# The last third of x loaded by SyncE in the loop's beginning instead of by GpSimd at the start, its statistics five slots later

## The chip, the cores and the metric

The kernel runs on one core of one Trainium2 chip. The metric is the device time of one execution in microseconds (us). Five engines work side by side: TensorE (PE; its weight loads are PEld), VectorE (DVE), ScalarE (ACT), GpSimd (POOL) and SyncE (SP), which here only issues DMAs. Each engine has its own program and waits for the others through semaphores. DMAs issued by SP travel in queue q1, those of ACT in q10, those of GpSimd in q0; all are carried by the core's 16 DMA engines.

## The reference, cut to what matters

x has 32 batches of 100 query rows of 256 values, the context 32 batches of 361 rows of 256.

```python
x = x + LN(z + LN0(x)) * gamma + beta      # z: 16-head cross attention of LN0(x) on ctx
x = x + FFN(LN0(x))                        # a second LN, top-2 of 8 experts (256-512-256, gelu), FFN adds its own input
LN0(x) = (x - mean(x)) / sqrt(var(x) + 1e-5)
```

What the change touches is the first LN0: every batch's rows of x must be in SBUF, and their mean and variance over 256 values computed, before the batch's queries are projected and, again, before its residual is added.

## The kernel before

Attention runs batch by batch as one software pipeline. A turn `i` has twelve slots `s` (`NG`), and in every slot each engine issues its share of up to five batches at once: batch i+3 is projected (keys L835, normalised rows L1099 and their transpose L845, queries L853), batch i+1 gets its value projection (L866), its score rows (L880) and their maxima (VectorE, L1344), batch i its transposed scores (L899), exponentials (L1163), a guard on VectorE (L1349) and the product with the values (L911); i-1 and i-2 get the end of attention and its layer norm. `pipeline()` runs i from -3; tables such as `DVE_PLACE` say in which slot a step stands. After the 32 batches, routing and the expert tiles follow (from about 560 us on).

Scores are computed in bfloat16 from a sum of products of parts. For each batch the queries and the keys are split into three parts (high on ACT, rest on GpSimd, middle on ACT, low on GpSimd: L748 to L771), and six DMAs each copy the parts into stacks of 96 rows: `q_stack<-q_part` (L624, for batch 0 L1238 on ACT) and `stack_x<-k_part` (L630). The stacks' last rows hold the row maxima, also in three parts; SyncE copies them there (L614) before the transposed scores (L899) of that batch. That copy is issued once per batch, from `m_part`, which ACT fills from a TensorE transpose (L890) of the parts `m_rows`.

x_all, behind the key stacks in the tensor `stack_x`, holds all of x. Four loads fill it (`X_LOADS`): batches 0 to 3 by ACT at the very start, 4 to 11 by SyncE behind the first weights and contexts (L589), 12 to 21 and 22 to 31 by GpSimd (L670), one behind the other, after the inverse deviations of batches 0 to 3. VectorE takes statistics (`x_sums`, one bn_stats a batch, L1280) and eight small steps turn them into a variance (`x_variance_step`, L1290 to L1304); GpSimd raises it to the power of -0.5 (`inverse_deviation_x`, L666), VectorE makes the offset (`x_offset`, L1313). This is done in three parts (`X_PARTS`): batches 0 to 3 before turn -3, 4 to 21 at the end of turn -2, and 22 to 31 in turns 0 to 2: the ten statistics stand one each in slots 0 to 9 of turn 0, the eight small steps in slots 1 to 8 of turn 1, the power at the end of GpSimd's turn 1, the offset at the end of turn 2. ACT waits for that offset before turn 4.

SyncE's program in its order: the first weights and contexts, L589, then for turn -3 batch 0's key stack copies, for turn -2 batch 1's query copies. At the start of turn -1 stands `later_loads()`: gamma and beta (L594, wanted by GpSimd in turn 2) and b1 (L595). The places of SyncE's table put batch 1's key copies (`k`, place 11) into turn -2 and so ahead of `later_loads()`. Behind it, in turn -1, stands the context of batch 3 (L607, wanted by the key projection in slot 5 of turn 0), in turn 0 the copy of batch 0's maxima (L614), and then batch 2's query and key copies.

Of the kernel before, what the change touches and what calls it, by code (L numbers as in the profile page):

```python
# [12 lines left out]
B, Q, D = 32, 100, 256  # L13
# [12 lines left out]
NG = G * KT  # L26
TINY = 1e-30
FIRST = 4
X_LOADS = [slice(0, FIRST), slice(FIRST, 12), slice(12, 22), slice(22, B)]
X_LATE = 22  # L30
TAIL_FROM = B - 2
X_PARTS = [slice(0, FIRST), slice(FIRST, X_LATE), slice(X_LATE, B)]
SCORES_LAG, GUARD_LAG, VALUES_LAG = 3, 6, 9
# [44 lines left out]
def after(eng, sem, value):  # L78

    if isinstance(value, int) and value <= 0:  # L80
        return
    eng.wait_ge(sem, value)


def lagging(turn, i, s, lag):

    return Batch(turn, i + (s - lag) // NG), (s - lag) % NG
# [13 lines left out]
def span_of(n, offset):  # L101

    if n.known and offset < 0 and n.index >= TAIL_FROM:
        return "tail"
# [24 lines left out]
def occupant_before(users, name, n):  # L129

    def at(user, index):
        offset, place = users[user]
        if n.known and offset < 0 and index >= TAIL_FROM:
            place = TAIL["PE"].get(user, place)
# [22 lines left out]
def build(nc, x, ctx_t, wq_t, bq, wk_t, bk, wv_t, bv, gamma, beta, ln_g, ln_b, rw, rb, w1, b1, w2, b2,  # L157
          ident_d, route_c, zscr, zf_d, odd_d, out):
    es = ExitStack()
    with es:  # L160
        def sem(name):
            return es.enter_context(nc.semaphore(name))
# [11 lines left out]
        x_all = stack_x[0:Q, stack_words:].rearrange("q (b d) -> q b d", b=B)  # L174
# [16 lines left out]
        x_loaded = [sem(f"x_loaded{k}") for k in range(4)]  # L191
# [272 lines left out]
        with att:  # L464
# [111 lines left out]
            def _(sp):  # L576
# [13 lines left out]
                sp.wait_ge(pad_written, 3)  # L590

                def later_loads():
                    for dst, src in zip(row_c, (gamma, beta)):
                        sp.dma_start(dst[:], src.unsqueeze(0).broadcast_to([Q, D])).then_inc(tail_const, 16)  # L594
                    sp.dma_start(b1_s[:], b1).then_inc(b1_loaded, 16)  # L595

                def iteration(turn, i):
                    if isinstance(turn, int) and i == -1:
                        later_loads()
# [52 lines left out]
            def _(pool):  # L652
# [10 lines left out]
                def inverse_deviation_x(k):  # L663

                    pool.wait_ge(ln0_step, 8 * (k + 1))
                    g.tensor_tensor(rstd0[:, X_PARTS[k]], ln0[0][:, X_PARTS[k]], half[:, 0:1].broadcast_to([Q, X_PARTS[k].stop - X_PARTS[k].start]), ALU.pow).then_inc(rstd0_ready, 1)  # L666

                inverse_deviation_x(0)
                for k in (2, 3):
                    pool.dma_start(x_all[:, X_LOADS[k], :], x.rearrange("b q d -> q b d")[:, X_LOADS[k], :]).then_inc(x_loaded[k], 16)  # L670

                gathers = [pool.alloc_register(f"gathers{k}") for k in range(2)]
                scatters = [pool.alloc_register(f"scatters{k}") for k in range(2)]
# [588 lines left out]
            def _(dve):  # L1262
# [15 lines left out]
                def x_sums(batches):  # L1278
                    for b in batches:
                        v.bn_stats(stats0[:, b, :], x_all[:, b, :]).then_inc(stats0_done, 1)  # L1280

                def x_variance_step(k, n):
                    part = X_PARTS[k]
                    me, mo = stats0[:, part, 1], stats0[:, part, 4]
                    l0, l1, l2 = (t[:, part] for t in ln0[0:3])
                    if n == 0:
                        dve.wait_ge(stats0_done, part.stop)
                    after(dve, ln0_step, 8 * k + n)
                    if n == 0:
                        v.tensor_tensor(l0, me, mo, ALU.add).then_inc(ln0_step, 1)  # L1290
                    elif n == 1:
                        v.tensor_scalar(mean0[:, part], l0, 0.5, None, ALU.mult).then_inc(ln0_step, 1)
                    elif n == 2:
                        v.tensor_tensor(l0, me, mo, ALU.subtract).then_inc(ln0_step, 1)
                    elif n == 3:
                        v.tensor_tensor(l1, l0, l0, ALU.mult).then_inc(ln0_step, 1)
                    elif n == 4:
                        v.tensor_tensor(l2, stats0[:, part, 2], stats0[:, part, 5], ALU.add).then_inc(ln0_step, 1)
                    elif n == 5:
                        v.tensor_scalar(l1, l1, 0.25, EPS, ALU.mult, ALU.add).then_inc(ln0_step, 1)  # L1300
                    elif n == 6:
                        v.tensor_scalar(l2, l2, 1.0 / D, None, ALU.mult).then_inc(ln0_step, 1)
                    else:
                        v.tensor_tensor(l0, l2, l1, ALU.add).then_inc(ln0_step, 1)  # L1304
# [168 lines left out]
                def iteration(turn, i):  # L1473
                    for s in range(NG):
# [6 lines left out]
                        n, g = lagging(turn, i, s, GUARD_LAG)  # L1481
# [4 lines left out]
                        if isinstance(turn, int) and i == -3 and s == 0:  # L1486
# [2 lines left out]
                            pad_stack(q_stack[ROWS:128].rearrange("r s h k -> r (s h k)"))  # L1489
                            for k in (1, 2):  # L1490
                                pad_stack(k_stack[ROWS:128, k].rearrange("r h k -> r (h k)"))
                        if isinstance(turn, int) and i == 0 and s < B - X_LATE:
                            if s == 0:
                                dve.wait_ge(x_loaded[3], 16)
                            x_sums(range(X_LATE + s, X_LATE + s + 1))
                        if isinstance(turn, int) and i == 1 and 1 <= s < 9:
                            x_variance_step(2, s - 1)
                        if isinstance(turn, int) and (i, s) == (-1, 0):
                            dve.wait_ge(route_const, 64)
                            for c in range(2):  # L1500
# [58 lines left out]
                        b = Batch(turn, i + 1)  # L1559
# [102 lines left out]
```

## Time and profile before

| | us |
|---|---|
| median of 3 runs | 878.26 (876.82 to 878.76) |
| the profiled execution | 875.23 |
| its span | 873.4 |
| TensorE busy | 751.5 (86%) |
| VectorE busy | 671.9 (77%) |
| GpSimd busy | 560.0 (64%) |
| ScalarE busy | 534.7 (61%) |

The span is the time between the first and the last instruction of the profiled execution; 1.8 us of its own time lie around it. Busy shares are means over the whole span. The page also cuts the span into 40 slices of 21.8 us and gives, for each, the busy tenths of every engine, TensorE's granted clock in tenths (PEclk, 9 being nearly full) and the DMA engines' share. A wait is charged to what ended it.

### The profile page before, as it was taken

Reading aid. Unit: us, or ns where it says so; the run is one execution under the profiler, and the core shown is the slowest. Engines: PE = TensorE matmul, PEld = TensorE weight load, DVE = VectorE, ACT = ScalarE, POOL = GpSimd, SP = SyncE. Lnnn points to the kernel's source line nnn. Section 1 sums busy time; section 2 is a strip of 40 time slices with the busy share of each in tenths; the row PEclk is TensorE's granted clock in tenths of the full one; section 3 lists DMA queues with packets and bytes.
Section 4 is the critical chain, followed back from the end, with each engine's and each line's share of the span. In section 5 each row is a group of like instructions: output and inputs, shape, how many; then the busy total and the mean of one; then the engine's idle time right before and its main releaser. Section 6 shows DMA issues by size and latency. Waiting matters only on the chain.

```text
span 873.4 us, 26128 instructions
## 1 busy us (share of the span) xinstructions
PE 751.5 (86%) x8056; PEld 584.9 (67%) x8057; DVE 671.9 (77%) x1855; ACT 534.7 (61%) x1412; POOL 560.0 (64%) x611
## 2 busy tenths in 40 slices
PE   3389999999999999999999988538786889999970
PEld 1256677777777777777777655427676779998960
DVE  7389999999999999999999977883468755555630
ACT  3246787888878888888887864425444345554520
POOL 6323877777777787777778754343755567777840
PEclk9699999999999999999999988757999999999995
DMA  8755576676776767758677687512342244443327
GB/s 198 141 131 121 129 166 151 161 172 149 175 163 148 180 152 165 173 139 188 138 176 164 154 247 204 142 34 43 60 60 43 45 67 68 67 61 57 64 36 150
DMA packets 154502, 110.95 MB, mean 127 GB/s; under 512 B 68688, under 2 KB 147884, under 8 KB 153920
## 3 DMA queue, kind: packets, MB, share of 16 engines
q1 hardware_dynamic: 132598, 77.01, 38.9%
q0 software_dynamic: 12192, 19.43, 13.5%
q10 hardware_dynamic: 9658, 13.85, 5.1%
q8 instruction: 28, 0.46, 0.2%
q14 instruction: 26, 0.21, 0.1%
HBM read 39.90 MB, written 23.88 MB: 73 GB/s over the span
## 4 chain that ended last, share of the span: by engine, by line
PE 62%; DVE 14%; issue 7%; DMA 5%; DVEq 4%; POOL 4%; ACT 1%; ACTq 1%; POOLq 0%; SPq 0%
PE pj L866 9%; PE pj L835 9%; PE s_row L880 9%; PE zt L911 8%; PE s_t L899 8%; PE s_row L970 5%; DVE negmax L1344 3%; PE pj L853 3%; PE zt L981 2%; PE pj L981 2%; DMA q_stack<-q_part 2%; DVE v_neg L1446 1%; DVEq L1441 1%; DVEq L1433 1%; PE tr L935 1%
## 5 line engine op out<-in xcount | busy, mean ns | idle before, releaser
L1344 DVE TENSOR_REDUCE negmax<-s_row 100x1 f32<-100x361 f32 x512 | 251.5, 524 | 25.9 <-PE s_row L880 18.9
L1163 ACT ACTIVATE p_t<-s_t 128x400 f32<-128x400 f32 x384 | 188.7, 501 | 61.7 <-PE s_t L899 55.4
L880 PE MATMUL s_row<-stack_x,q_stack 125*128 125x361 bf16 x512 | 133.2, 323 | 14.5 <-DMA q_stack<-q_part 7.9
L899 PE MATMUL s_t<-q_stack,stack_x 128*128 128x100 bf16 x1536 | 129.6, 212 | 14.7 <-ACT p_t L1163 10.5
L899 PEld LDWEIGHTS s_t<-q_stack,stack_x 128*128 128x128 bf16 x1536 | 93.6, 100 | 61.8 <-issue 27.0
L970 PE MATMUL s_row<-w_qkv,v_aug 128*128 128x128 f32 x912 | 115.6, 281 | 15.4 <-DVE v_aug L1435 15.4
L970 PEld LDWEIGHTS s_row<-w_qkv,v_aug 128*128 128x128 f32 x912 | 109.5, 197 | 18.4 <-DVE v_aug L1435 16.5
L866 PE MATMUL pj<-w_qkv,ct 128*128 128x256 f32 x384 | 107.4, 403 | 0.0
L835 PE MATMUL pj<-ct,w_qkv 128*128 128x361 f32 x256 | 94.9, 494 | 10.3 <-DMA bk_s<-in_bk 9.2
L1149 ACT ACTIVATE w_qkv<-s_row,b_k 128x128 f32<-128x128 f32 x228 | 64.9, 368 | 62.5 <-PE s_row L970 62.5
L1349 DVE TENSOR_SCALAR p_t<-p_t 128x1200 f32<-128x1200 f32 x128 | 100.9, 789 | 0.3 <-ACT p_t L1163 0.2
L911 PE MATMUL zt<-p_t,v_aug 128*32 128x100 f32 (+1 forms) x3072 | 97.4, 260 | 1.7 <-DVE p_t L1349 1.0
L911 PEld LDWEIGHTS zt<-p_t,v_aug 128*32 128x32 f32 (+1 forms) x3072 | 67.7, 112 | 28.8 <-issue 24.9
L688 POOL DMA_INDIRECT q_part<-zf_d,idx_g x57 | 64.4, 1130 | 22.8 <-issue 15.0
L880 PEld LDWEIGHTS s_row<-stack_x,q_stack 125*128 125x128 bf16 x512 | 48.1, 102 | 45.8 <-DVE negmax L1344 25.4
L698 POOL DMA_INDIRECT out_x<-v_neg,idx_s x29 | 49.9, 1719 | 35.4 <-DVE v_neg L1448 25.7
L866 PEld LDWEIGHTS pj<-w_qkv,ct 128*128 128x128 f32 x384 | 67.4, 195 | 6.2
L698 POOL DMA_INDIRECT odd_d<-v_neg,idx_s x28 | 48.2, 1723 | 29.8 <-DVE v_neg L1448 22.8
L776 POOL TENSOR_TENSOR u<-z_in,td 100x256 f32<-100x256 f32 x32 | 45.9, 1433 | 31.0 <-DMA z_in<-zscr 21.2
L835 PEld LDWEIGHTS pj<-ct,w_qkv 128*128 128x128 f32 x256 | 45.5, 196 | 27.2 <-issue 10.4
L1435 DVE TENSOR_SCALAR v_aug<-w_s 128x1024 f32 x57 | 40.4, 708 | 27.2 <-issue 24.9
L779 POOL TENSOR_TENSOR rstd<-var,half 100x1 f32<-100x1 f32 x32 | 33.1, 1035 | 43.8 <-DVE var L1384 43.8
(234 smaller groups left out, 1482.1 us busy)
## 6 DMA issues: line engine op xcount, KB each, us to landing
stack_x<-k_part SPq DMA_DIRECT2D x192, 192.0 KB, 3.8
q_stack<-q_part SPq DMA_DIRECT2D x186, 64.0 KB, 2.0
ct<-in_ctx_t SPq DMA_DIRECT2D x32, 361.0 KB, 5.0
stack_x<-in_w ACTq DMA_DIRECT2D x8, 512.0 KB, 6.4
w_s<-in_w ACTq DMA_DIRECT2D x14, 256.0 KB, 3.1
zscr<-zn SPq DMA_DIRECT2D x32, 100.0 KB
z_in<-zscr SPq DMA_DIRECT2D x32, 100.0 KB
zf_d<-zf_s SPq DMA_DIRECT2D x32, 100.0 KB
```

The lines of the kernel that those rows point to most:

```text
L688: pool.indirect_dma_start(zg[:, k.ring, :], None, zf_rows[0:n], bass.IndirectOffsetOnAxis(idx_g[:, k.ring:k.ring + 1], 0), bounds_check=n ...
L698: pool.indirect_dma_start((out_rows, odd_rows)[k.slot][0:n], bass.IndirectOffsetOnAxis(idx_s[:, k.slot:k.slot + 1], 0), ys[:, k.slot, :], ...
L835: last = nc.tensor.matmul(pj[1][:, 0:KEYS], wk_s[:, c, t * 128:t * 128 + 128], ct[:, a.slot, c, 0:KEYS], start=(c == 0), stop=(c == 1))
L866: last = nc.tensor.matmul(bank[:, kt % 2 * D:kt % 2 * D + D], ct[:, b.slot, c, kt * 128:kt * 128 + 128], wv_s[:, c, :], start=(c == 0), st ...
L880: nc.tensor.matmul(s_row[h % 2][:, 0:KEYS], q_stack[0:MROW, b.slot, h, :], k_stack[0:MROW, b.slot, h, 0:KEYS], start=True, stop=True).then ...
L899: last = nc.tensor.matmul(s_t[g % 2][:, j * Q:j * Q + Q], k_stack[:, b.slot, h, kt * 128:kt * 128 + 128], q_stack[:, b.slot, h, 0:Q], star ...
L911: last = nc.tensor.matmul(zt[32 * j:32 * j + 32, quad * Q:quad * Q + Q], v_aug[0:n, b.slot, kt * H + 4 * quad + j, :], p_t[0:n, quad % 2, ...
L970: last = nc.tensor.matmul(p_h[k.slot][:, j * 128:j * 128 + 128], w1_k[k.slot][:, c * HF + j * 128:c * HF + j * 128 + 128], zgt[:, k.slot, ...
L1149: nc.scalar.activation(hidt[:, k.slot, j * 128:j * 128 + 128], p_h[k.slot][:, j * 128:j * 128 + 128], ACT.Gelu, bias=b1_k[:, k.slot, j:j + ...
L1163: nc.scalar.activation(p_t[:, quad % 2, kt, :], s_t[g % 2][:, 0:4 * Q], ACT.Exp).then_inc(exp_done, 1)
L1344: v.tensor_reduce(negmax[:, b.slot, h:h + 1], s_row[h % 2][0:Q, 0:KEYS], AXIS.X, ALU.max, negate=True).then_inc(max_done, 1)
L1349: v.tensor_scalar(p_t[:, quad % 2], p_t[:, quad % 2], 0.0, None, ALU.max).then_inc(p_ready, 1)
```

## The change

Load 3 (x of batches 22 to 31, 1000 KB) is issued by SyncE as the first thing of `later_loads()`, no longer by GpSimd. Its ten statistics and the wait for the load move from slots 0 to 9 of turn 0 to slots 5 to 11 of turn 0 and 0 to 2 of turn 1. The eight small steps move from slots 1 to 8 to slots 4 to 11 of turn 1. GpSimd's power and the offset stay at the ends of turns 1 and 2.

```diff
+X_SLOT = 5
...
                 def later_loads():
+                    sp.dma_start(x_all[:, X_LOADS[3], :], x.rearrange("b q d -> q b d")[:, X_LOADS[3], :]).then_inc(x_loaded[3], 16)
                     for dst, src in zip(row_c, (gamma, beta)):
...
                 inverse_deviation_x(0)
-                for k in (2, 3):
-                    pool.dma_start(x_all[:, X_LOADS[k], :], x.rearrange("b q d -> q b d")[:, X_LOADS[k], :]).then_inc(x_loaded[k], 16)
+                pool.dma_start(x_all[:, X_LOADS[2], :], x.rearrange("b q d -> q b d")[:, X_LOADS[2], :]).then_inc(x_loaded[2], 16)
...
-                        if isinstance(turn, int) and i == 0 and s < B - X_LATE:
-                            if s == 0:
+                        if isinstance(turn, int) and 0 <= i * NG + s - X_SLOT < B - X_LATE:
+                            n = X_LATE + i * NG + s - X_SLOT
+                            if n == X_LATE:
                                 dve.wait_ge(x_loaded[3], 16)
-                            x_sums(range(X_LATE + s, X_LATE + s + 1))
-                        if isinstance(turn, int) and i == 1 and 1 <= s < 9:
-                            x_variance_step(2, s - 1)
+                            x_sums(range(n, n + 1))
+                        if isinstance(turn, int) and i == 1 and 4 <= s < 12:
+                            x_variance_step(2, s - 4)
```

## Rows read from the trace of the kernel before

**Rows 1.** The page: span, busy times, TensorE's granted clock in 40 slices.
```profile
span 873.4 us, 26128 instructions
PE 751.5 (86%) x8056; PEld 584.9 (67%) x8057; DVE 671.9 (77%) x1855; ACT 534.7 (61%) x1412; POOL 560.0 (64%) x611
```

**Rows 2.** Timeline, 29 to 60 us: start, duration, engine, line, operation [idle before <-releaser].
```profile
29.24 3.37 DVE L1280 BATCH_NORM_STATS2 stats<-stack_x 100x6 f32<-100x256 f32 x10 [7.98 <-DMA stack_x<-in_x]
...
34.87 3.30 POOL L666 TENSOR_TENSOR rstd<-ln,half 100x18 f32<-100x18 f32 x1 [0.97 <-DVE ln L1304]
...
41.51 0.78 PE L880 MATMUL s_row<-stack_x,q_stack 125*128 125x361 bf16 x2 [7.93 <-DMA q_stack<-q_part]
...
42.21 3.81 SPq L630 DMA_DIRECT2D stack_x<-k_part  x6
...
47.49 0.60 SPq L607 DMA_DIRECT2D ct<-in_ctx_t  x1
...
55.47 0.47 PE L880 MATMUL s_row<-stack_x,q_stack 125*128 125x361 bf16 x2
...
56.80 0.85 SPq L614 DMA_DIRECT2D q_stack<-m_part  x1
...
59.11 0.53 PE L899 MATMUL s_t<-q_stack,stack_x 128*128 128x100 bf16 x8
```

**Rows 3.** ACT's six query stack copies of batch 0 (L1238), issue to landing.
```profile
DMA to landing us min/median/max: 8.2/11.3/15.7
```

**Rows 4.** DMA queues, 14 to 18, 18 to 22, 22 to 26 us: packets, MB, share.
```profile
q0 software_dynamic: 233, 0.32, 46.0%
...
q0 software_dynamic: 165, 0.68, 101.5%
...
q0 software_dynamic: 205, 0.55, 103.3%
q1 hardware_dynamic: 6, 0.01, 3.8%
```

**Rows 5.** GpSimd's two loads of x (L670), from their issue at 10.8 and 13.5 us.
```profile
DMA to landing us min/median/max: 18.4/21.8/25.2
```

**Rows 6.** DMA queues, 38 to 41.5 us.
```profile
DMA packets 542, 0.36 MB, mean 103 GB/s; under 512 B 65, under 2 KB 541, under 8 KB 541
```

**Rows 7.** Busy us by stretch: PE, PEld, DVE, ACT, POOL, granted clock, DMA share, GB/s.
```profile
41.50:47.30 5.80, 5.74 (x16) 3.74 (x16) 3.23 (x7) 0.34 (x1) 0.68 (x1) 0.51 0.71 165
...
59.10:68.00 8.90, 7.11 (x76) 4.55 (x75) 8.79 (x22) 4.87 (x13) 1.66 (x2) 1.00 0.79 182
68.00:75.00 7.00, 7.00 (x72) 5.02 (x69) 5.95 (x12) 5.37 (x14) 3.95 (x5) 1.00 0.18 48
```

**Rows 8.** The context load of batch 3 (L607), issue to landing.
```profile
DMA to landing us min/median/max: 4.5/4.5/4.5
```

**Rows 9.** DMA traffic, 12.5 to 15 (batches 4 to 11 of x), 43 to 52, 50 to 51.5 us.
```profile
DMA packets 475, 0.38 MB, mean 153 GB/s; under 512 B 104, under 2 KB 475, under 8 KB 475
...
q1 hardware_dynamic: 371, 0.38, 69.6%
...
DMA packets 1500, 1.77 MB, mean 197 GB/s; under 512 B 276, under 2 KB 1500, under 8 KB 1500
...
DMA packets 333, 0.35 MB, mean 235 GB/s; under 512 B 92, under 2 KB 333, under 8 KB 333
```

**Rows 10.** TensorE's timeline: a value projection at the low and the high clock.
```profile
42.09 1.91 PE L866 MATMUL pj<-w_qkv,ct 128*128 128x256 f32 x4
...
54.60 1.03 PE L866 MATMUL pj<-w_qkv,ct 128*128 128x256 f32 x4
```

**Rows 11.** Timeline, 83 to 88 us, VectorE and GpSimd.
```profile
83.32 0.39 DVE L1304 TENSOR_TENSOR ln<-ln 100x10 f32<-100x10 f32 x1
...
87.21 2.49 POOL L666 TENSOR_TENSOR rstd<-ln,half 100x10 f32<-100x10 f32 x1
```

## The prediction

> **What bounds the kernel now.** I read the page first: TensorE is busy 86% of a span of 873.4 us, and its 40 slices are full but for the first ones [rows 1]. A batch in the steady part is out of reach of a load that runs once, so only the start can change. I then read the timeline of the first 100 us, the landings and the DMA queues in short windows.
>
> TensorE's score rows of batch 0 start at 41.51 us, after 7.93 us of waiting for the copies of q_part into q_stack [rows 2]. ACT's six copies take 8.2 to 15.7 us to land [rows 3]. The cause stands in the queues: from 18 to 26 us the engines carry GpSimd's queue at 101.5 and 103.3%, SyncE's at 3.8% in the second half, where its stack copies are issued [rows 4]. Of GpSimd's two loads of 1000 KB one lands after 18.4 us (the ten statistics at 29.24 show it) and the other after 25.2 us, near 38.7 [rows 2, 5]. The second is the load that the change moves. From 38 to 41.5 us only 103 GB/s flow [rows 6]: the few engines that still shared their time with that load work off their copies.
>
> The next thing is which wait ends last *after* 41.5 us. Batch 1's score rows begin at 55.47, and the first transposed scores of batch 0 at 59.11; SyncE issues the small copy of the maxima that these wait for at 56.80 [rows 2]. VectorE is busy 8.79 of 8.9 us from 59.1 on and sets the pace there; then TensorE does, 7.00 of 7 us [rows 7].
>
> **The change part by part.** The sum is against the profiled execution, 875.23 us; the median of the three runs is 878.26, 3.0 higher, and I carry the difference over to it.
>
> *Load 3 leaves the beginning.* Both loads together are 2.05 MB; GpSimd's queue moved 0.32 MB from 14 to 18 us and 0.68 in the next 4 [rows 4]. Alone, load 2 has 0.7 MB left at 18 us: 4 to 8 us, so it lands at 22 to 26, not 29.2. The last of batch 0's twelve stack copies was issued 15.7 us before 41.4, at 25.7. They then have the engines to themselves and land near 34 to 35 (bounds 33 and 38): the first score row starts 6 to 7 us earlier. GpSimd's issue of 2.2 us goes too, on an engine that then idles.
>
> *What of that reaches batch 1.* Its key copies are issued at 42.21, behind the chain: ten statistics, eight small steps, GpSimd's power of 18 columns (34.87, 3.30 us), k_rest, k_mid, k_low [rows 2]. GpSimd had waited 0.97 us for the steps. With load 2 early the power starts at 33.9, 1.0 us earlier, and no more, since what GpSimd does ahead of it hangs on ACT, which issues copies until 26.4. So batch 1's key copies go out at 41.2.
>
> *Load 3 in SyncE's queue.* It is 1.02 MB ahead of gamma, beta, b1, batch 3's context and, as it turns out, the copy of batch 0's maxima. SyncE's own issue grows by about 0.5 us, hidden, since the queue behind is backlogged. The context load goes out at 47.49 and lands 4.5 us later, at 52.0 [rows 2, 8]; the queue is empty until 56.80. The trace doesn't show this load in this place, so I bound it: at the 235 GB/s of the end of that backlog 4.4 us; at the 153 GB/s of the load of batches 4 to 11, same form and queue, 6.7 us [rows 9]. The whole backlog ran at 197, which gives 5.2. I take 6.0, nearer to the load of the same form. Then the context lands at 52.0 - 1.0 + 6.0 = 57.0 and the small copy, issued near 50 now, right behind it, about 57.4. The key copies of batch 1, ahead of load 3, land by about 49 (the context behind them in before landed at 52.0), and the slots from batch 1's first score row to those scores took 3.6 us (55.5 to 59.1), so TensorE would be ready at 52 to 53. So the start's 6 to 7 us shrink to 59.1 - 57.4 = 1.7 us.
>
> Against the change speaks that the load of batches 4 to 11 held the engines at 69.6% only, the work of 11 of 16 [rows 9]: SyncE's load doesn't use them all, so the full-width rates may not hold for it.
>
> The Trainium skill (DMA: Bandwidth & Descriptors, "Why a DMA increments its semaphore by 16 and not by 1") says that a load issued from SyncE runs on the largest number of engines up to 16 that divides its slowest dimension, so ten for 100 partitions, and those the lowest. The trace agrees within one engine. By the rule with the backlog's rate, ten sixteenths of 197 GB/s, the load would take 8.3 us and the sum below would be +1.4 us.
>
> *The new idle time of TensorE.* It waits some 5 us before 57.4. After 7.9 us without a matmul the granted clock was at its low level of 1.2 GHz (0.51), for 5.8 us of work, and 1.00 from 59.1 on [rows 2, 7]. At the low level two value projections (x4) took 1.91 us, at the high one 1.03 [rows 10]; score rows suffer less, so I take 1.7 times. In 3 to 5.8 us of low clock that adds 1.3 to 2.4 us to the 7.11 us of TensorE work of that stretch: 8.4 to 9.5 against 8.9 [rows 7].
>
> *The statistics.* Ten take 3.37 us, 0.34 each [rows 2]. Five leave slots 0 to 4 of batch 0's turn; five go to slots 10, 11 and the first three of the next turn. In the stretch from 59.1 VectorE loses two of them, 0.7 us, and what it still owed at 59.11, an estimated 1.2 us (two row maxima and a bias add): 6.9 of its 8.79 are left [rows 7], so TensorE sets that stretch. I take +0.2 us for it, with the clock. From 68 to 75 us VectorE idles 1.05 us and gets up to 1.7 us of statistics, less the first small steps, which move on: I take 0.3 us for what finds no gap there.
>
> *The small steps, three slots later.* The last one ran at 83.32, and GpSimd's power of ten columns started at 87.21, held by nothing but its order [rows 11]. Now the last step stands in slot 11, three slots on, about 87.5 at some 1.4 us a slot, so the power starts about 0.3 us later, with k_rest behind it: +0.3.
>
> Sum: -1.7 + 0.2 + 0.3 + 0.3 = -0.9 us: 874.3 for the profiled execution, 877.4 for the median. A difference under 0.2% (1.75 us) is what a measurement of this kernel can't tell from none.
>
> **The rivals.**
>
> *The start's gain survives (faster).* If the maxima's copy isn't held behind load 3, the scores start near 53 and 6 us are kept, less 0.6 for the rest: 872.9. If it is held but load 3 takes only 4.4 us, the head gains 3.3, the idle time is shorter, and about 2.5 us are kept: 875.8. For it speaks the full rate after the backlog; against the first form, that every copy of SyncE before 52.0 landed in the order of issue.
>
> *The wait moves and brings the low clock (slower).* Its place is TensorE's wait for the maxima's copy. At 69.6% of the backlog's 197 GB/s load 3 takes 7.5 us and the head gains only 0.2; TensorE then idles over 6 us and has the low clock for 6 us of work or more, which costs 2 us in place of 0.2: 878.3 - 0.2 + 2.0 + 0.6, about 880.7. It decides from 7 us of load 3 on, or from a low clock longer than 6 us.
> The Trainium skill's rule on the number of engines (DMA: Bandwidth & Descriptors, the section named above) speaks for this rival.
>
> *Nothing to gain, since the engines carry the same bytes.* The stack copies run on the same engines, so taking 1.02 MB from one place and putting it in another gives back later what it gives now: 878.3. From the rows it needs a first score row still near 38 and a context load later by all of 6 us.
> The Trainium skill has it as a rule (DMA: Bandwidth & Descriptors, "Issuing engines are not separate DMA queues"): queues of several engines interleave on the same 16, and another issuer saves its issue time alone. From 22 to 26 us the trace doesn't agree: SyncE's queue has copies to carry and gets 3.8%.
>
> **How the numbers follow.** My forecast and the third rival both end within 0.2%: 0.42. The first rival: 0.38, most of it in its second form and in shifts of a microsecond that fall on that side. The second: 0.20. The range takes the bounds: 4.4 us for load 3 with little clock loss gives 874; a bit of the surviving start takes it to 873.5; 7.5 us and the long low clock end at 880.6.
>
> **What would show it.** Right: the first score row near 34 to 35; batch 1's key copies issued near 41; load 3 issued behind them; the maxima's copy issued near 50 but landing near 57; TensorE idle from 52 on, waiting for that copy; a second stretch of low granted clock after it; batch 4's k_rest 0.3 us late behind the power. Wrong: a first score row still at 38 or later; scores of batch 0 starting within 2 us of the issue of the maxima's copy; a granted clock of 1.00 through 50 to 70 us, which with a short load 3 would make it clearly faster; statistics that wait for load 3.

## The result, and the profile after

The change made the kernel slower, by a little. The median is 878.15 us over 22 runs (875.89 to 879.82), that of the kernel before, run beside it, 876.16 (869.13 to 878.76): a ratio of 1.0032, 95% interval [1.0018, 1.0046]. A second set gave 1.0056 [1.0035, 1.0078]. The forecast was 0.1% faster (877.4). The profiled execution took 879.75 us.

The page after: span and busy times; only the span moved [rows 1].
```profile
span 877.9 us, 26128 instructions
...
PE 754.9 (86%) x8056; PEld 587.6 (67%) x8057; DVE 670.7 (76%) x1855; ACT 534.8 (61%) x1412; POOL 558.3 (64%) x610
```

The timeline after, 25 to 65 us, with the columns of [rows 2]:
```profile
26.03 3.37 DVE L1281 BATCH_NORM_STATS2 stats<-stack_x 100x6 f32<-100x256 f32 x10 [4.82 <-DMA stack_x<-in_x]
...
34.98 0.47 PE L881 MATMUL s_row<-stack_x,q_stack 125*128 125x361 bf16 x2
...
42.76 1.22 SPq L632 DMA_DIRECT2D stack_x<-k_part  x2
...
46.61 0.54 SPq L594 DMA_DIRECT2D stack_x<-in_x  x1
...
49.63 0.60 SPq L609 DMA_DIRECT2D ct<-in_ctx_t  x1
...
51.15 0.85 SPq L616 DMA_DIRECT2D q_stack<-m_part  x1
...
53.09 0.47 PE L881 MATMUL s_row<-stack_x,q_stack 125*128 125x361 bf16 x2
...
59.71 0.85 PE L900 MATMUL s_t<-q_stack,stack_x 128*128 128x100 bf16 x8 [6.15 <-DMA q_stack<-m_part]
...
61.82 2.77 PE L836 MATMUL pj<-ct,w_qkv 128*128 128x361 f32 x4 [0.66 <-DMA ct<-in_ctx_t]
```
Read it from the top. Load 2 is in 3.2 us earlier (26.03 for 29.24), the first score row starts 6.5 us earlier. Then load 3 goes out at 46.61, the context of batch 3 and the copy of the maxima behind it, and TensorE stands from 53.6 to 59.7, waiting for that 9.4 KB copy. Before, it had those scores at 59.11. A gain of 6.5 us has become a loss of 0.6.

The landing of the contexts loaded in the loop (L609) after: the longest is batch 3's, 12.1 us where it took 4.5 [rows 8].
```profile
DMA to landing us min/median/max: 4.0/4.9/12.1
```

Busy times by stretch after, columns of [rows 7] (the granted clock is the third from the end):
```profile
54.00:58.00 4.00, 0.00 (x0) 0.00 (x0) 0.76 (x2) 0.00 (x0) 0.00 (x0) 0.73 0.81 210
58.00:62.00 4.00, 1.63 (x11) 0.98 (x12) 1.10 (x3) 1.14 (x3) 0.00 (x0) 0.50 1.12 230
62.00:66.00 4.00, 4.00 (x15) 2.19 (x15) 0.94 (x3) 0.60 (x2) 0.00 (x0) 0.50 0.98 204
66.00:70.00 4.00, 3.42 (x38) 2.16 (x41) 4.00 (x10) 3.15 (x9) 0.57 (x1) 0.99 0.11 30
```
The clock's low level falls on the first work after the wait. GpSimd's timeline after, 87 to 92 us, where [rows 11] had the power at 87.21:
```profile
88.57 1.01 POOL L740 TENSOR_TENSOR m_rows<-m_rest,m_rows 100x16 bf16<-100x16 f32 x1
89.88 2.42 POOL L668 TENSOR_TENSOR rstd<-ln,half 100x10 f32<-100x10 f32 x1 [0.31 <-DVE ln L1305]
```

The power now waits 0.31 us for the last small step, as expected; of its 2.7 us of delay 2.2 are the delay of the whole pipeline (batch 2's maxima are transposed at 89.99 for 87.75).

The ledger. These starts, in us, are read from TensorE's timelines of the profiled executions; "in the gap" is the kernel *gap_late* of the experiments.

| start of | before | change | in the gap |
|---|---|---|---|
| first score row | 41.5 | 35.0 | 34.7 |
| batch 0's transposed scores | 59.1 | 59.7 | 53.0 |
| transpose of batch 1's maxima | 71.9 | 74.4 | 65.4 |
| of batch 3's maxima | 104.4 | 107.6 | 98.6 |
| of batch 31's maxima | 549.8 | 552.1 | 544.0 |
| end of the span | 873.4 | 877.9 | 868.1 |

Change against before: +0.6 at the scores, +2.0 up to batch 1's maxima, +0.7 over the next two batches, -0.9 over the other 28. That last figure is spread between traces: the second traces of both kernels have 445.1 us there. The expert part has +2.2 us, and that too is not the change's: it comes in two lengths, about 324 and 326 us from batch 31's maxima to the end. The change had 325.8 in one trace and 324.2 in another, the kernel before 323.6 and 325.9.

### The profile page after: what moved, and what is told of

The parts are those of the page before. It is cut to its first block, busy times and chain, and to the rows that moved or that the text cites. A ratio compares the mean times of both kernels' runs of the same rounds, so it can differ in the third digit from the quotient of the medians.

```text
span 877.9 us, 26128 instructions
## 1 busy us (share of the span) xinstructions
PE 754.9 (86%) x8056; PEld 587.6 (67%) x8057; DVE 670.7 (76%) x1855; ACT 534.8 (61%) x1412; POOL 558.3 (64%) x610
## 4 chain that ended last, share of the span: by engine, by line
PE 62%; DVE 13%; issue 7%; DMA 6%; POOL 4%; DVEq 4%; ACT 2%; SPq 1%; ACTq 1%; POOLq 0%
PE pj L836 9%; PE pj L867 9%; PE s_row L881 8%; PE zt L912 8%; PE s_t L900 8%; PE s_row L971 6%; PE pj L854 3%; PE pj L982 3%; DVE negmax L1345 2%; PE zt L982 2%; DMA q_stack<-m_part 1%; DVE v_neg L1447 1%; DMA ct<-in_ctx_t 1%; DVEq L1434 1%; DVEq L1442 1%
## 5 line engine op out<-in xcount | busy, mean ns | idle before, releaser
L1164 ACT ACTIVATE p_t<-s_t 128x400 f32<-128x400 f32 x384 | 188.5, 501 | 68.4 <-PE s_t L900 62.5
L971 PE MATMUL s_row<-w_qkv,v_aug 128*128 128x128 f32 x912 | 118.0, 285 | 13.7 <-DVE v_aug L1436 13.7
L971 PEld LDWEIGHTS s_row<-w_qkv,v_aug 128*128 128x128 f32 x912 | 111.7, 200 | 16.7 <-DVE v_aug L1436 14.9
L836 PE MATMUL pj<-ct,w_qkv 128*128 128x361 f32 x256 | 96.3, 500 | 10.9 <-DMA bk_s<-in_bk 9.1
L867 PE MATMUL pj<-w_qkv,ct 128*128 128x256 f32 x384 | 104.8, 395 | 0.5 <-ACT k_rest L1087 0.5
L777 POOL TENSOR_TENSOR u<-z_in,td 100x256 f32<-100x256 f32 x32 | 48.1, 1504 | 30.5 <-DMA z_in<-zscr 21.3
L836 PEld LDWEIGHTS pj<-ct,w_qkv 128*128 128x128 f32 x256 | 46.0, 198 | 28.8 <-issue 10.9
L765 POOL TENSOR_TENSOR k_rest<-k_rest,k_part 128x722 f32<-128x722 f32 x32 | 51.7, 1614 | 16.0 <-ACT k_rest L1087 16.0
```

The costliest lines, as they stand in the source:

```text
L836: last = nc.tensor.matmul(pj[1][:, 0:KEYS], wk_s[:, c, t * 128:t * 128 + 128], ct[:, a.slot, c, 0:KEYS], start=(c == 0), stop=(c == 1))
L867: last = nc.tensor.matmul(bank[:, kt % 2 * D:kt % 2 * D + D], ct[:, b.slot, c, kt * 128:kt * 128 + 128], wv_s[:, c, :], start=(c == 0), st ...
L971: last = nc.tensor.matmul(p_h[k.slot][:, j * 128:j * 128 + 128], w1_k[k.slot][:, c * HF + j * 128:c * HF + j * 128 + 128], zgt[:, k.slot, ...
L1164: nc.scalar.activation(p_t[:, quad % 2, kt, :], s_t[g % 2][:, 0:4 * Q], ACT.Exp).then_inc(exp_done, 1)
```

## The experiments

Theory A: the start's gain is real, and load 3 gives it back, since its packets hold the engines that the maxima's copy and batch 3's context need next; the loss beyond zero comes from those two waits and the low clock behind them. Rivals: the order of SyncE's queue alone; the late statistics and the late power; the clock. In the first expectations theory A goes by the name of bytes theory, and the order of SyncE's queue by that of ring theory. In the cuts of the edits "..." stands for lines left out; wherever load 3 gets a new line, its line in `later_loads()` goes. All ratios are to the kernel before, run on the same chip, with 95% intervals.

### The change a second time


> The changed kernel itself, on the chip of the next three. Ring theory (load 3 stands ahead of batch 3's context and of batch 0's maxima copy in SyncE's queue): as in the first profile, transposed scores of batch 0 near 59.7 us though their copy is issued near 51, a low granted clock from 56 to 66 us, and 1.002 to 1.005 of the kernel before. Statistics theory (the later statistics cost the time): the same ratio. Bytes theory (the 16 engines carry the same bytes, wherever they are issued): the same ratio.

878.59 us, 1.0056 [1.0035, 1.0078]. Transposed scores of batch 0 at 60.8, the transpose of batch 1's maxima at 74.8, of batch 3's at 108.0: the pattern repeats. Its first score row stands at 37.7, not 35.0; what made that is told in the last section.

### Statistics alone
Both loads back on GpSimd, everything else as changed:
```diff
-                    sp.dma_start(x_all[:, X_LOADS[3], :], ...)
...
-                pool.dma_start(x_all[:, X_LOADS[2], :], ...)
+                for k in (2, 3):
+                    pool.dma_start(x_all[:, X_LOADS[k], :], ...)
```


> The kernel before with the change's statistics and small steps in their later slots alone; both loads stay with GpSimd. In the change and in three other kernels with late small steps, batch 3's maxima are transposed 17.5 to 17.6 us after batch 2's, where the kernel before has 16.6. If the later small steps delay GpSimd's power and key rest of batch 4 (statistics theory, as one part), the same interval shows 17.6 here, with the head as before (first transposed scores at 59), and the ratio is 1.001. If the interval came from the shifted loads, it stays at 16.6 and the ratio is 0.999 to 1.000.

874.43 us, 0.9999 [0.9977, 1.0022]. The late statistics and steps cost nothing that shows in the time. Batch 0's scores to batch 3's maxima take 45.0 us here (55.88 to 100.86) and 45.2 in both traces of the kernel before. The loss is load 3's.

### Load 3 behind the maxima's copy
```diff
+                        if isinstance(turn, int) and (i, s) == (-1, 7):
+                            sp.dma_start(x_all[:, X_LOADS[3], :], ...)
...
-X_SLOT = 5
+X_SLOT = 8
...
```
The small steps start two slots later, two at a time at first.

> Load 3 still issued by SyncE, but behind batch 3's context and batch 0's maxima copy; statistics from slot 8 of turn 0. Ring theory: the context lands near 52, the maxima copy within 3 us of its issue at 51, transposed scores of batch 0 near 53 to 54, no low clock after 50 us, and 5 to 6 us less than the kernel before: ratio 0.993 to 0.995. Bytes theory: load 3 then delays batch 2's stack copies or something else by as much, so the ratio stays at 1.000 or above. Statistics theory: they are later still, so 1.003 or more.

875.81 us, 1.0031 [1.0005, 1.0057]. TensorE's timeline, 52 to 70 us:
```profile
52.97 0.53 PE L901 MATMUL s_t<-q_stack,stack_x 128*128 128x100 bf16 x8
...
64.04 0.35 PE L901 MATMUL s_t<-q_stack,stack_x 128*128 128x100 bf16 x4 [1.46 <-ACT p_t L1165]
...
69.11 0.76 PE L882 MATMUL s_row<-stack_x,q_stack 125*128 125x361 bf16 x2 [2.85 <-issue]
```
The copy lands at 53.0, 2.3 us after its issue, and the scores start 6.7 us sooner than in the change. But load 3, now in flight from 52 to 62, holds batch 2's stack copies: the last of its key copies lands at 69.0, where TensorE's next score row starts (the trace calls that wait "issue"). The wait has moved one batch on.

### Load 3 from ACT's queue
```diff
+                        if isinstance(turn, int) and (i, s) == (-1, 9):
+                            act.dma_start(x_all[:, X_LOADS[3], :], ...)
...
```


> Load 3 issued by ACT in slot 9 of turn -1 (near 45 us), in a queue of its own, with SyncE's queue as in the kernel before. Ring theory: it shares the engines packet by packet and holds nobody up for its whole length: batch 3's context lands by 54 to 55, the maxima copy within 3 us of its issue, scores of batch 0 at 53 to 55, ratio 0.993 to 0.997. Bytes theory: same bytes at the same time as in the change, so the copy waits as long and the ratio is 1.003. Statistics theory: 1.003.

878.03 us, 1.0052 [1.0030, 1.0075]. SyncE's queue holds no load 3, yet TensorE waits longer than in the change. Its timeline, and the DMA queues from 50 to 60 us:
```profile
62.21 0.85 PE L899 MATMUL s_t<-q_stack,stack_x 128*128 128x100 bf16 x8 [8.76 <-DMA q_stack<-m_part]
```
```profile
q1 hardware_dynamic: 1250, 0.97, 44.0%
q10 hardware_dynamic: 961, 0.98, 39.5%
```
The two queues share the engines, and both are slower for it: load 3's thousand packets, issued at 47.7, were in flight for 11.2 us (51.0 to 62.2), and batch 3's context took 12.2 us to land.

### The maxima's copy from ACT's queue
```diff
...
+                            if b.known and b.index == 0:
+                                act.wait_ge(m_copied, 1)
+                                act.dma_start(q_stack[MROW:MROW + 3, 0, :, 0:Q], m_part[:]).then_inc(m_stacked[0], 16)
```


> The change, with the small copy of batch 0's maxima issued by ACT (which has just written m_part) instead of by SyncE; load 3 stays where the change has it. Theory A (load 3's thousand packets of 1 KB keep the ten lowest engines busy whatever queue the copy travels in, as the load in ACT's queue suggested): the copy still lands near 58 to 62, TensorE's wait of 6 us stays, batch 1's maxima at 73.5 to 75, ratio 1.002 to 1.006. Theory B (the copy is held by the order of SyncE's queue): it lands near 54, the transposed scores start near 54 to 55, batch 3's context, still behind the load, then ends a wait near 60, ratio 0.998 to 1.002.

879.10 us, 1.0042 [1.0022, 1.0061]. The timeline, 50 to 61 us:
```profile
50.31 0.85 ACTq L1221 DMA_DIRECT2D q_stack<-m_part  x1
...
60.49 0.85 PE L902 MATMUL s_t<-q_stack,stack_x 128*128 128x100 bf16 x8 [7.78 <-DMA q_stack<-m_part]
```
A copy of 9.4 KB, alone in its queue, takes 10 us. (SyncE, which no longer waits for the maxima, issues batch 2's query copies from 49.46 instead of 52.05, so a little more competes with it than in the change.) With the run before, the order of SyncE's queue falls as the cause: what counts is what the engines already hold, whichever queue it came from. Here the Trainium skill's rule (DMA: Bandwidth & Descriptors, "Issuing engines are not separate DMA queues") agrees with the traces: another issuer brings no other carrier.

### Load 3 as 96 and 4 partitions
```diff
+                    for rows in (slice(0, 96), slice(96, Q)):
+                        sp.dma_start(x_all[rows, X_LOADS[3], :], ...)
...
```


> The change with load 3 as two DMAs of SyncE, of 96 and 4 partitions. If the load's 8 us are those of ten engines carrying 100 packets each (partitions 100), the first part spreads over 16 and takes about 5 us: the maxima copy lands 2 to 3 us earlier (56.5 to 57.5), and the ratio falls by 0.002 to 0.004, to about 1.000. If the memory side sets the 145 GB/s of the load, its length stays at 8 us and the ratio at 1.003.

876.61 us, 1.0037 [1.0018, 1.0056]; batch 1's maxima are transposed at 73.1, 1.7 us before the change run beside it. The trace's semaphore events tell how many engines carried a load. Uncut, load 3 leaves ten landings in the first trace of the change, from 56.2 to 58.1 us; the piece of 96 partitions leaves sixteen, from 54.3 to 55.0. The uncut load shows in the context behind it too: six of its sixteen landings come at 53.5 to 53.8, the other ten from 58.3 on. So load 3 sits on ten engines. Spreading it makes it about 2 us shorter (its last four partitions land at 56.4) but puts it in front of everything on all sixteen: the maxima's copy still landed at 59.4, for 59.7 and 60.7 in the two traces of the change. Against the change run beside it 1.3 of the 1.7 us are that wait (59.45 for 60.76) and 0.4 the stretch behind it, where the context came at 60.0, not 62.5. The two traces of the change differ by as much from each other, and the ratios overlap, so no gain of the cut is shown.

### Matmuls in place of the wait
```diff
...
+                        for _ in range(FILL):
+                            nc.tensor.matmul(s_t[1][:, 0:KEYS], q_stack[0:ROWS, 0, 0, :], k_stack[0:ROWS, 0, 0, 0:KEYS], start=True, stop=True)
```


> The change with 32 extra matmuls on TensorE (into a bank that the next scores overwrite) while it waits for batch 0's maxima copy. Clock theory: the granted clock stays at 1.00 from 50 to 70 us, transposed scores start near 59.7 as in the change, but batch 1's maxima are transposed 1.5 to 2 us earlier than in it (near 73) and the ratio falls by 0.002 against the change. If the wait alone costs the time, batch 1's maxima stay near 74.7 and the ratio stays at 1.003 to 1.005.

1.0034 [1.0015, 1.0053], and it told nothing: TensorE still waited 1.43 and 1.28 us, and the clock fell all the same, from 62 to 69 us. Mended, with 36 before the scores and 14 before batch 3's key projection:

> The change, with 36 matmuls that nobody reads (about 0.16 us each, 5.7 us) before batch 0's transposed scores and 14 more (2.2 us) before the key projection of batch 3; their banks are overwritten by the next real work. TensorE is then busy up to the landing of the maxima's copy and of batch 3's context, and the earlier filler's mistake (1.43 and 1.28 us of waiting were left) is mended. Theory A (about half of what is lost against before comes from the low clock after the wait): no granted clock under 0.9 from 50 to 75 us, batch 1's transposed maxima at 72.5 to 73.5 where the change has 74.5 to 74.9, and the whole 1 to 2 us under the change, ratio to before about 1.003. Theory B (VectorE paces that stretch, the clock costs nothing): batch 1's maxima at 74.5 or later with full clock, ratio as the change's, 1.003 to 1.006. If the clock falls all the same, the question stays open.

877.40 us, 1.0032 [1.0013, 1.0050]. Busy times by stretch, to be read against the change's:
```profile
54.00:58.00 4.00, 4.00 (x28) 2.54 (x26) 1.38 (x3) 0.00 (x0) 0.58 (x1) 1.00 0.84 210
58.00:62.00 4.00, 3.51 (x30) 2.18 (x28) 1.09 (x3) 1.15 (x3) 0.00 (x0) 1.00 1.04 221
62.00:66.00 4.00, 3.59 (x25) 2.21 (x24) 1.46 (x4) 1.40 (x4) 0.00 (x0) 1.00 1.05 217
```
The clock is at 1.00 throughout. Whether that saved anything is read from batch 3's key projection, which waits for the context. Here it starts at 63.01, 0.5 us after the context landed (62.49), since the fourteen matmuls ran over:
```profile
63.01 1.38 PE L841 MATMUL pj<-ct,w_qkv 128*128 128x361 f32 x4
...
73.90 0.23 PE L896 MATMUL tr<-ident_bf,m_rows 100*48 100x100 bf16 x1
```
The stretch from batch 0's transposed scores to the transpose of batch 1's maxima, cut at the start of that projection, in us:

| kernel | clock behind the scores | scores to projection | projection to batch 1's maxima |
|---|---|---|---|
| before | full | 1.84 | 10.90 |
| *stats_only* | full | 1.51 | 10.90 |
| *gap_late* (below) | full | 1.52 | 10.91 |
| *filler2* | full | 2.82 | 10.89 |
| change | low | 2.11 | 12.59 |
| change, second trace | low | 1.80 | 12.27 |
| *ctx_first* (next) | low | 1.25 | 12.22 |

The second part is 10.9 us wherever the clock is full, *filler2* with its late context among them, and 12.2 to 12.6 where it is low. (The other kernels with a low clock there, full or in part, have 11.9 to 12.9.) So the low clock costs the change 1.4 to 1.7 us. Less the 0.5 us that the matmuls ran over, batch 1's maxima would stand at 73.4, which is theory A's figure. The time of the whole kernel doesn't resolve it: 1.0032 here, 1.0032 and 1.0056 for the change.

### Batch 3's context ahead of load 3
```diff
+                        if isinstance(turn, int) and (i, s) == (-1, 6):
+                            sp.dma_start(x_all[:, X_LOADS[3], :], ...)
                         for m in due(turn, i, s, 1, "SP", "max"):
...
```


> The change, with load 3 one place later in SyncE's program: behind the context of batch 3, still ahead of the copy of batch 0's maxima. Theory A (of the 14.7 us from the first transposed scores to batch 1's maxima about 1.3 us are the wait for the context, 0.5 the low clock): the context lands by 54, the key projection of batch 3 waits for nothing, the maxima's copy lands late as before (60 to 63), and that stretch shrinks to 13 to 13.5 us; ratio 1.001 to 1.005. Theory B (the context's wait hides behind VectorE's work): the stretch stays at 14.0 to 14.8 us although the context is early.

879.46 us, 1.0058 [1.0039, 1.0076]. TensorE's timeline, 53 to 66 us:
```profile
62.16 0.85 PE L901 MATMUL s_t<-q_stack,stack_x 128*128 128x100 bf16 x8 [8.68 <-DMA q_stack<-m_part]
62.81 0.81 PE L882 MATMUL s_row<-stack_x,q_stack 125*128 125x361 bf16 x2
63.41 2.61 PE L837 MATMUL pj<-ct,w_qkv 128*128 128x361 f32 x4
```
The context is there by 53.9 and nothing waits for it; from the scores at 62.16 to batch 1's maxima at 75.63 it takes 13.5 us, as A said. The table above splits A's sum otherwise than A did: the wait for the context is 0.3 to 0.9 us (2.11 and 1.80 in the change for 1.52 in *gap_late* and 1.25 here), and the low clock the larger part. The change's 14.7 us are *gap_late*'s 12.4, 0.6 for the wait and 1.7 for the clock, the second trace's 14.1 are 12.4, 0.3 and 1.4. These are differences between single traces, good to some tenths.

The run shows one thing more. The maxima's copy was issued at 51.07, as in the change (51.15), but load 3 went out 2.1 us later (48.67 for 46.61), and the copy landed 2.4 us later, at 62.1: its landing follows the load, not its own issue.

### Load 3 in the gap
SyncE issues load 3 behind batch 0's key copies, with the statistics and the power in the slots of before:
```diff
+                        if isinstance(turn, int) and (i, s) == (-2, 0):
+                            sp.dma_start(x_all[:, X_LOADS[3], :], ...)
...
-                for k in (2, 3):
-                    pool.dma_start(x_all[:, X_LOADS[k], :], ...)
+                pool.dma_start(x_all[:, X_LOADS[2], :], ...)
```


> The kernel before with load 3 moved to SyncE's queue behind batch 0's key copies (issue near 27 us), where the engines of the changed kernel idle from 33 to 43; statistics in their old slots. Bytes theory (a load costs what it delays on the lowest ten engines, wherever it is issued): it lands by 41, delays no copy that anyone waits for, first score rows near 35, transposed scores of batch 0 at 53 to 54, no low clock behind them, ratio 0.993 to 0.995. Ring theory: batch 1's copies stand behind it but have 7 us to spare, so the same. If the start is given back by some other wait, batch 3's maxima are transposed at 104.5 as before and the ratio is 1.000.

870.83 us, 0.9973 [0.9953, 0.9992]: faster, from where the change is slower. With the small steps and the power moved forward as well:

> gap_sp with the small steps right behind the statistics (slots 10 of turn 0 to 2 of turn 1) and GpSimd's power of ten columns in slot 3 of turn 1, where it idles for 7 us. Statistics theory: the interval between the transposes of the maxima of batches 2 and 3 falls from 16.6 to about 15.6, and the ratio by another 0.001, to 0.992 to 0.994.

871.22 us, 0.9958 [0.9939, 0.9976], the same within the intervals. The power's move alone, in the kernel before:

> The kernel before, loads and statistics untouched, with the eight small steps of batches 22 to 31 in slots 10 and 11 of turn 0 and 0 to 2 of turn 1 and GpSimd's power in slot 3 of turn 1 instead of at that turn's end. Theory A (the power's place is worth little): ratio 0.998 to 1.001, maxima of batch 3 within 0.5 us of before's 104.5. Theory B (the power at the turn's end holds up k_rest of batch 4 on the path): interval from batch 2's to batch 3's maxima down from 16.6 to about 15.7, ratio 0.997 to 0.999. The change's own interval there was 17.6.

875.16 us, 0.9994 [0.9974, 1.0014]. The batch 2 to 3 interval fell from 16.6 to 15.8 us, as B said, but that from 1 to 2 rose from 15.9 to 17.2, where the power now stands. It costs wherever it is.

### The change with one line moved
As *gap_sp*, with the change's own slots:

> The change with one line moved: SyncE issues load 3 behind batch 0's key copies (near 27 us) and no longer behind batch 1's, with the change's own slots for statistics and small steps. Against the kernel that had this load in this place with the slots of before (0.9973) it shows what the late slots cost once the load is out of the way. Theory A (place of the load is the whole matter): load 3 lands near 41, batch 0's transposed scores start near 53, batch 1's maxima at 65.5 to 66.5, batch 3's near 99, ratio 0.996 to 0.999. Theory B (the late statistics and the later power cost a microsecond or more of their own): batch 3's maxima at 100 or later, ratio 0.999 to 1.001.

869.86 us, 0.9931 [0.9906, 0.9955]. The timeline, 26 to 54 us:
```profile
27.00 0.87 SPq L604 DMA_DIRECT2D stack_x<-in_x  x1
...
34.69 0.47 PE L882 MATMUL s_row<-stack_x,q_stack 125*128 125x361 bf16 x2
...
49.77 0.47 PE L882 MATMUL s_row<-stack_x,q_stack 125*128 125x361 bf16 x2 [2.61 <-issue]
...
53.00 0.53 PE L901 MATMUL s_t<-q_stack,stack_x 128*128 128x100 bf16 x8
```
Busy times by stretch, first of *gap_late*, then of the change; the DMA share is the last column but one:
```profile
30.00:34.00 4.00, 4.00 (x20) 3.01 (x19) 0.16 (x1) 2.02 (x6) 0.40 (x1) 1.00 0.78 155
34.00:38.00 4.00, 3.55 (x19) 2.57 (x19) 2.35 (x6) 1.76 (x4) 3.52 (x3) 1.00 0.70 171
38.00:42.00 4.00, 2.67 (x12) 1.17 (x10) 3.16 (x7) 1.60 (x3) 3.08 (x3) 1.00 0.25 58
```
```profile
30.00:34.00 4.00, 4.00 (x19) 2.89 (x18) 1.40 (x9) 2.06 (x6) 0.08 (x1) 1.00 0.25 45
34.00:38.00 4.00, 3.52 (x17) 2.58 (x17) 2.08 (x5) 1.76 (x4) 3.52 (x3) 1.00 0.13 33
```
In the change the engines are nearly idle from 31 to 42 us; the same load, put there, is over by 39, and nothing waits for it. The score row, the scores and the copies keep their early places. The same load, with the same ten landings, costs nothing here and the whole gain of the start when issued 20 us later. A second time:

> The change with load 3 behind batch 0's key copies, a second time on another draw of chip and runs. If the gain is real: 868 to 871, ratio 0.991 to 0.996, and the same start (first score row at 34.3 to 34.8, first transposed scores near 53, batch 3's maxima near 98.7).

870.03 us, 0.9955 [0.9938, 0.9972]: the gain repeats. Cut into 96 and 4 partitions:

> The kernel with load 3 in the gap, cut into 96 and 4 partitions, so that the large piece can use all 16 engines. Theory A (in the gap the load delays nothing, so its length does not matter): it ends 2 to 3 us sooner than the 41 of the uncut one, and the time is the same, 868.5 to 871, ratio 0.991 to 0.996. Theory B (its packets still compete with batch 0's stack copies when they use all engines): first score row at 35.5 or later, ratio 0.996 or more.

869.30 us, 0.9946 [0.9924, 0.9968]: the same time, so in the gap its length doesn't matter. Its first score row came at 38.0 us, which fits B's figure, but TensorE was busy without a pause from 28.6 us up to it, with the second key projection at 2.75 us, as in the second trace of the change (last section), and the transposed scores came only 1.1 us later than in *gap_late*: it was not the copies that held it.

### The kernel before, traced again


> The kernel before itself, for a second trace. Theory A (the start varies with how GpSimd's loads and the stack copies share the engines): first score row at 38.5 to 41.6 us, time in proportion, 871 to 876; ratio 0.998 to 1.002. Theory B (the start is always the same and the spread of the runs comes from the tail): first score row at 41.5 within 0.3 us.

875.10 us, 1.0004 [0.9975, 1.0032]. TensorE's timeline:
```profile
41.78 0.48 PE L880 MATMUL s_row<-stack_x,q_stack 125*128 125x361 bf16 x1 [8.71 <-DMA q_stack<-q_part]
...
59.34 0.53 PE L899 MATMUL s_t<-q_stack,stack_x 128*128 128x100 bf16 x8
```
First score row at 41.78, transposed scores at 59.34, batch 3's maxima at 104.6: the trace that the forecast was built on was no odd one. *stats_only* and *pow_only*, with the same two loads at the start, both had that row at 38.9, so this start has two forms; which runs take which was not settled.

## Why the prediction was wrong

*Load 3 leaves the beginning.* Right: load 2 landed at 26.0, at the end of the 22 to 26 us expected, and the first score row started at 35.0. The reason for that time was only partly right. Batch 0's query copies took 3.6 to 5.7 us, so they were in by 32.7, and then TensorE's own work, 4.00 of 4 us from 30 to 34, came last.

*What reaches batch 1.* Wrong: its key copies were issued at 42.76, not 41.2. GpSimd's power started at 35.48, not at 33.9, with no wait in front of it. What GpSimd does ahead of it hangs on ACT, as the forecast said, but ACT issued its last copy of batch 0 at 27.01, not 25.73, and everything behind it moved with it. In *gap_late* the key copies went out at 42.44, so load 3's place is not what delayed them.

*Load 3 in SyncE's queue.* **This is the first step that failed.** The forecast took 6.0 us for load 3 and had the maxima's copy land at 57.4. In the gap, with next to nothing in its way, its thousand packets of 1 KB were in flight from 30.4 to 38.0 us: 7.6 us, 134 GB/s. In the change it also went out later, at 46.61 behind the key copies, where the forecast's figures make it about 45.1. The maxima's copy landed at 59.7 (60.7 in the second trace), and the context at 61.8, not 57.0. So the head, forecast 1.7 us ahead of before, was 0.6 behind. The copy's own issue (51.15 for "near 50") is no part of it: issued at 50.31 by ACT it landed at 60.5. The copy came 1.6 and 2.9 us after the last piece of load 3 in the two traces; what fills that rest was not separated. The rows had said the length: at 69.6% of 197 GB/s, from the load of the same form [rows 9], it is 7.5 us. The forecast quoted that row and then took a value between it and the full-width rate.
The Trainium skill (DMA: Bandwidth & Descriptors, "Why a DMA increments its semaphore by 16 and not by 1") has the engines of a load of 100 partitions as ten, and the traces agree, with their ten landings. The estimate made from that count and the backlog's rate, 8.3 us, was nearer than 6.0.

*The low clock and the statistics behind it.* **The second step that failed**: +0.2 us taken, +2.0 measured. The cost of the clock itself was about right, 1.3 to 2.4 us forecast and 1.4 to 1.7 measured in the change's two traces. What failed is the overlap that should have hidden it. The forecast let TensorE's 7.11 us of work set a stretch of 8.9 once some statistics had left VectorE and the idle time had let it catch up. With the late statistics at full clock the stretch to batch 1's maxima only fell from 12.74 to 12.4 us (*stats_only*, *gap_late*), and behind the key projection it did not fall at all: 10.9 us also in *filler2*, where VectorE had idled first. The forecast also left out the second wait behind the same load, batch 3's context, worth 0.3 to 0.9 us, though it had worked out both landings.

*The late statistics and the late power.* +0.6 us taken, +0.7 measured in the trace over batches 1 to 3, but by other terms. From batch 0's scores to batch 3's maxima, the late slots save 0.3 us whichever way load 3 is issued: 45.0 (*stats_only*) for 45.2 (before), 45.6 (*gap_late*) for 45.9 (*gap_sp*). The late steps, with the power behind them, do cost about what was forecast, 0.4 us between the maxima of batches 2 and 3 (16.98 for 16.60), and the late statistics give back 0.3 in each of the two intervals before. What is left is 0.6 us that came with moving the load, in a term that nobody had. GpSimd's subtraction for the queries' rest, ahead of batch 3's maxima, before and after:
```profile
100.41 0.56 POOL L771 TENSOR_TENSOR q_rest<-q_rest,q_part 128x200 f32<-128x200 f32 x1
```
```profile
103.24 1.96 POOL L772 TENSOR_TENSOR q_rest<-q_rest,q_part 128x200 f32<-128x200 f32 x1 [0.18 <-issue]
```
It takes 1.96 us in all fourteen traces of kernels that took load 3 out of GpSimd's program, wherever they put it, and 0.56 in the four traces that left it there. Why it is longer stays open.

*The rivals.* The outcome is the second rival's in mechanism: the wait moved to the maxima's copy, load 3 took over 7 us, the low clock followed. Its +2.4 us against the median of before stands beside measured +2.0 and, in the second set, +4.5. Its price of 2 us for the clock was near the 1.4 to 1.7 measured; it had the head gain 0.2 us where it lost 0.6, and it too lacked the wait for the context. "Nothing to gain, the engines carry the same bytes" fell with the first score row at 35 and, for good, with the load in the gap. The absolute range held the time (878.15 in 873.5 to 880.6), but that is luck: the kernel before ran 2 to 4 us under the median that the forecast started from. Against the kernel run beside it the change is 2.0 and 4.5 us slower, where 0.9 faster was forecast.

## What to carry to other kernels

A load moved off a crowded stretch is worth only what its new place leaves of the gain: look for the stretch of the DMA share column that is nearly empty (0.13 to 0.27 here) and issue it there, not merely "later"; one line's place made the difference between 1.003 to 1.006 and 0.993 to 0.996. Idle time behind such a wait has a second price, the low clock of the work after it, and slack that is to hide it must be shown at full clock first. Ask for every transfer what small copy will be issued within its length behind it, on any queue, and price the load by its form (engines used, packet size), not by the rate of the mixed traffic around it.

## What the runs showed of the hardware

A load of 100 partitions by 10 rows of 1 KB used ten of the sixteen engines; a packet took 73 ns (median) in the gap and 75 in the crowded place, and 100 of them on each engine make most of the 7.6 us for 1.02 MB. A copy of 9.4 KB issued into that, even from an empty queue, took 10 us (*max_by_act*), and 2.3 without it (*gap_late*).

In the change's traces the record of the granted clock does not tell TensorE's speed at the start. Timelines of the change, of its first and its second run; both clocks are granted at 1.00 from 26 to 38 us:
```profile
28.92 2.66 PE L836 MATMUL pj<-ct,w_qkv 128*128 128x361 f32 x4
...
32.82 1.46 PE L836 MATMUL pj<-ct,w_qkv 128*128 128x361 f32 x4
```
```profile
28.77 2.66 PE L836 MATMUL pj<-ct,w_qkv 128*128 128x361 f32 x4
...
33.45 2.75 PE L836 MATMUL pj<-ct,w_qkv 128*128 128x361 f32 x4
...
37.70 0.56 PE L881 MATMUL s_row<-stack_x,q_stack 125*128 125x361 bf16 x2
```
After 9.4 us without a matmul a key projection took 2.66 us, as it does at the low level (2.77 at 0.50, at 61.82 us in the change). In the first run the second projection was back at 1.46 us, in the second run still at 2.75; with the shorter work around it, that puts the first score row at 35.0 or at 37.7. *act_queue* has the same durations as the second run (2.66 and 2.75 us), and there the record says 0.50 from 26 to 36 us. By the transposed scores 1.1 us of the 2.7 are left.
